# Twelve token tiles: all layer norms and transposes first, then all K and V projections

## The reference

```python
x = x + layernorm(attn(layernorm(x)))
x = x + layernorm(ffn(layernorm(x)))

# attn: 32 heads of 128 dimensions, ONE key head and ONE value head
Q = x @ Wq.T;  K = x @ Wk.T;  V = x @ Wv.T      # Wk, Wv: (128, 4096)
Qr, Kr = rope(Q), rope(K)
out = sliding_window(sigmoid scores, normalised; window 512, half overlapping, blended)
return out @ Wo.T
# ffn: x @ base_W.T + routed low-rank terms (8 experts, top 2, rank 16)
```

## Time and profile before

| | us |
|---|---|
| median of 3 runs | 2727.24 |
| lowest, highest | 2717.52, 2794.48 |
| the profiled execution | 2714.36 |
| its span on the slowest core (core 1) | 2712.8 |
| spans of the 8 cores | 2693.8 to 2712.8 |
| TensorE busy, of the span | 2003.1 (74%) |
| ScalarE busy | 659.5 (24%) |
| VectorE busy | 578.5 (21%) |

### The profile page before, as it was taken

How to read it: one execution, slowest core, us unless ns; L and a number is a source line. 1 busy time by engine, 2 the same in 40 slices (tenths; PEclk the granted TensorE clock), 3 DMA queues, 4 the chain that set the end, 5 groups by cost and what they waited for, 6 DMA issues and landing times.

```text
span 2712.8 us, 50094 instructions; the slowest of 8 cores (2693.8 to 2712.8 us)
## 1 busy us (share of the span) xinstructions
PE 2003.1 (74%) x20000; PEld 1720.9 (63%) x20000; DVE 578.5 (21%) x1656; ACT 659.5 (24%) x1159; POOL 135.7 (5%) x194
## 2 busy tenths in 40 slices
PE   1444599999998777788899999931222699999910
PEld 1333499999976555566688888831212588888810
DVE  1222222222213334433200000034332000000045
ACT  1434211111125554545211111132332011111122
POOL 1000000000000000000000000001101100000000
PEclk9556799999996888867899999965555799999965
DMA  9522044565561000000356475512111755755445
GB/s 182 121 94 93 32 63 63 70 84 66 63 78 18 2 2 2 2 2 2 18 72 85 63 92 65 75 50 62 41 53 32 89 73 67 91 69 72 73 140 217
DMA packets 228592, 179.01 MB, mean 66 GB/s; under 512 B 18960, under 2 KB 222736, under 8 KB 222736
## 3 DMA queue, kind: packets, MB, share of 16 engines
q0 software_dynamic: 217568, 113.35, 33.3%
q1 hardware_dynamic: 10800, 62.45, 6.4%
HBM read 263.97 MB, written 25.17 MB: 107 GB/s over the span
## 4 chain that ended last, share of the span: by engine, by line
PE 67%; issue 9%; DVE 9%; ACT 7%; DMA 6%; POOL 1%; DVEq 1%; ACTq 0%; POOLq 0%; SPq 0%
PE ps_all L814 17%; PE ps_all L670 17%; PE ps_all L455 16%; PE ps_all L557 7%; DVE bn L264 4%; PE ps_all L505 2%; DMA xre<-x_ext 2%; ACT sig L519 2%; DMA wvT_s<-wvT 2%; ACT xt_stage L283 2%; PE ps_all L296 2%; DMA x1re<-x_scratch 1%; DVE bl L593 1%; PE ps_all L351 1%; PE ps_all L356 1%
## 5 line engine op out<-in xcount | busy, mean ns | idle before, releaser
L814 PE MATMUL ps_all<-slab,ln2T 128*128 128x256 bf16 x4096 | 463.7, 273 | 22.2 <-DMA brider<-b_all 22.2
L455 PE MATMUL ps_all<-slab,ln1T_own 128*128 128x256 bf16 x4096 | 467.9, 273 | 0.7 <-ACT krT L380 0.7
L670 PE MATMUL ps_all<-slab,attn_T 128*128 128x256 bf16 x4096 | 449.6, 273 | 1.0 <-ACT attn_T L631 1.0
L814 PEld LDWEIGHTS ps_all<-slab,ln2T 128*128 128x128 bf16 x4096 | 402.0, 98 | 69.9 <-issue 22.4
L670 PEld LDWEIGHTS ps_all<-slab,attn_T 128*128 128x128 bf16 x4096 | 401.8, 98 | 48.8 <-issue 1.2
L455 PEld LDWEIGHTS ps_all<-slab,ln1T_own 128*128 128x128 bf16 x4096 | 395.4, 98 | 44.3 <-issue 0.8
L519 ACT ACTIVATE sig<-ps_all,kbias_s 128x512 bf16<-128x512 f32 x384 | 225.5, 719 | 244.6 <-PE ps_all L505 244.3
L557 PE MATMUL ps_all<-v_sb,sig 128*128 128x128 bf16 x2048 | 237.7, 245 | 45.4 <-DVE bl L593 40.4
L557 PEld LDWEIGHTS ps_all<-v_sb,sig 128*128 128x128 bf16 x2048 | 224.8, 125 | 57.0 <-issue 56.9
L567 PE MATMUL ps_all<-onesc,sig 128*128 128x1 bf16 x2048 | 232.5, 190 | 0.0
L567 PEld LDWEIGHTS ps_all<-onesc,sig 128*128 128x128 bf16 x2048 | 193.7, 101 | 0.0
(11 more groups left out here) (90 smaller groups left out, 1585.7 us busy)
## 6 DMA issues: line engine op xcount, KB each, us to landing
slab<-wqT POOLq DMA_DIRECT2D x16, 2048.0 KB, 18.6
slab<-woT POOLq DMA_DIRECT2D x16, 2048.0 KB, 17.0
slab<-baseT POOLq DMA_DIRECT2D x16, 2048.0 KB, 14.7
xstage<-x_ext SPq DMA_DIRECT2D x12, 2048.0 KB, 7.7
out<-outstage SPq DMA_DIRECT2D x8, 2048.0 KB, 7.9
xre<-x_ext POOLq DMA_DIRECT2D x8, 1024.0 KB, 8.2
x_scratch<-x1b SPq DMA_DIRECT2D x8, 1024.0 KB, 3.9
x1re<-x_scratch SPq DMA_DIRECT2D x8, 1024.0 KB, 9.7
```

The lines of the kernel that those rows point to most:

```text
L455: return e.matmul(reg, ln1T_own[:, d, t * 128:(t + 1) * 128], slabs[par][:, d, :], start=(d == 0), stop=(d == 31))
L670: return e.matmul(reg, attn_T[:, d, t * 128:(t + 1) * 128], slabs[par][:, d, :], start=(d == 0), stop=(d == 31))
L814: return e.matmul(reg, ln2T[:, d, t * 128:(t + 1) * 128], slabs[par][:, d, :], start=(d == 0), stop=False)
```

## The change

The one loop becomes two: all 12 a(ti) stand first, then all 12 b0(ti). `xt_stage` moves up by 8192 bytes, so that it no longer lies on `ln1T_halo`; it now lies on the first bytes of `v_sb` and on the rotary buffers `km1` and `km2`, which b0 alone writes. From L386 on, line numbers shift (the query tables' L393 becomes L392).

```diff
-    xt_stage  = sb("xt_stage", (128, D), BF16, FREG + 24576)
+    xt_stage  = sb("xt_stage", (128, D), BF16, FREG + 32768)
...
-    for ti in range(NTX + 1):
-        if ti >= 1:
-            emit_b0(ti - 1)
-        if ti < NTX:
-            emit_a(ti)
+    for ti in range(NTX):
+        emit_a(ti)
+    for ti in range(NTX):
+        emit_b0(ti)
```

## The result

Over ten executions each, the changed kernel has a median of 2659.3 us (lowest 2652.1) and the kernel before one of 2724.5 us (lowest 2716.4). The ratio is 0.9777, with a 95% interval of 0.9737 to 0.9817: faster, though this interval alone leaves open whether by 2%. By it the change makes the kernel faster by 66 us, 2.4%. The forecast was 2640 us, 77.7 us less, with a range of 2618 to 2678.

What follows compares the result with a forecast made beforehand. It saw a chain of engines waiting on each other before the first query matmul: layer norms to 187.9 us, then K and V of 59.7, put that matmul at 247.7, not 325.42; 77.7 less gives 2640 us (2618 to 2678).

Steps and rivals of the forecast that it cites:

- The chain, and the statistics hidden: Layer norm stage: VectorE's next statistics run under ScalarE's apply and evacuations, so the period falls from 24.3 to 11.61 us.
- x late beside the slabs: Layer norms of tiles 2 to 5: x loads slowed by query weight slabs make ScalarE wait 13.2 us in all.
- The slabs 10 us later: Query weight loads: x takes its share earlier, so the second slab lands some 10 us after the former 96.2.
- K and V in one go: TensorE after the last transposes: first block 7.16 us, eleven more at 2.4 GHz of 4.78 each, 59.7 in all.
- The first query matmul: Start of the query projection: it comes at 247.7 us instead of 325.42.
- From there to the whole: Everything behind the first query matmul: order, waits and loads stay as before, so the whole 77.7 us gain reaches the end.
- the clock doesn't hold: Rival, K and V blocks: all run at 1.2 GHz, 36.3 us more, a gain of 41, 2676 us; chance 0.13.
- x becomes the bound: Rival, layer norm stage: x loads stay at contended speed to the end, up to 2751 us; chance 0.03.
- the loads aren't late: Rival, layer norm stage: x arrives in time, the 13.2 us of waits go, gain 90.9, 2627 us; chance 0.18.

## Why the prediction was right, point by point

- **The chain, and the statistics hidden.** Right. The period without late loads is 11.4 us (11.61 forecast). Held back, the statistics cost 48 us; moved alone, they bring 56.
- **x late beside the slabs.** Right in place and cause, and in size on core 1: 13.2 us forecast for tiles 2 to 5, of which 6.0 for tile 2; 15.7 measured on core 1, of which 7.0 for tile 2. The chosen 14 us a load, between bounds of 7.7 and 20, came as 14.0, 14.4 and 15.1. On the other cores the loads came less evenly, and the sum was 12.2 to 20.3 us; that it came so near on the core whose rows were read is in part luck. With the slabs away all of it goes. By the rule of the Trainium skill that a DMA engine goes round its queues packet by packet (page "DMA: Bandwidth & Descriptors", section "Queues, rings and completion order"), weighed in the prediction as one turn for each packet of the profile, a load would have taken an estimated 9 us. The trace doesn't agree with that weighing; whether a turn of the rule is one packet of the profile, no run here shows.
- **The slabs 10 us later.** Too small: the second slab was issued at 44.1 and landed 72.4 us later, at 116.5 on core 1, 20 us after the 96.2 of before. It was due only at the second slab's matmuls and nobody waited for the slab itself.
- **K and V in one go.** Right: first K matmul at 187.0 (187.2 forecast), and the clock is up from 1.1 us on. The first block took 5.4 us (192.41, where the next K matmul starts, less 186.97) instead of 7.2, because the step fell after 1.1 us, not five; the later blocks take 5.10 on the mean (from the transposition at 192.18 to the eleventh after it, at 248.32: 56.1 / 11) instead of 4.78. Of the difference most lies behind the second transposition, 0.39 us to the next K matmul (197.15 to 197.54, part of it marked as issue) where I had put one step of 0.056. Behind the first block it is 0.18 (192.23 to 192.41), behind ten later ones 0.39 each; why, no run shows. In the trace of before the next tile's layer norm stood there.
- **The first query matmul** on core 1: 249.2, forecast 247.7. Up to here the sum holds within 2 us, in part by luck: x is 2.5 us later than forecast, but the eleven periods are 2.6 us shorter together; the first K and V block is 1.7 us shorter, the eleven others together 3.5 longer.
- **From there to the whole: the step that failed.** "All of it reaches the end" holds for core 1, which gained 76 us at the first query matmul and 80 at its end. But 77.7 was the gain of the core whose rows I read, not that of the kernel. On cores 1 and 2 K waited for the V weights until 53.7 and 54.5; on the six others it started between 45.6 and 48.2, so they had reached the query projection 5 to 10 us ahead of core 1 and had less to gain: 69.5 us on the mean. Core 4, which began its query projection 7 us ahead of core 1, ended the profile of before level with it at 2712.8: its query projection took 483.0 us, core 1's 477.3, so which core ends last is decided later. So the measure of the stage is its mean over the cores. That accounts for 8.2 of the 11.7 us between 77.7 and 66.0; the other 3.5, not seen in the profiled executions, belong to executions without a trace and stay open.
- **Rivals.** That the clock doesn't hold and that x becomes the bound didn't happen; that the loads aren't late is what the kernel with late slabs made of it: 2627.6, where 2627 stood as the price. That the two agree so closely is in part chance: it is one execution, and its Q is 86.4 us earlier than before on the mean, where 90.9 stood.

## What to carry to other kernels

In a list that an engine runs strictly in order, look first for work that is ready but stands behind a wait: here three VectorE lines, moved ahead of the rotary step, carry four fifths of the gain of regrouping the whole loop. Packing such a chain brings its loads closer together, so look at once for what else fills the DMA engines then and isn't due yet. On several cores price a stage as its mean over the cores; the rows of the slowest core may hold a wait that the others don't have.

## What was not expected

- The record of the granted clock says nothing before its first entry, which on core 1 is a rise: at 59.4 us before, at 188.1 in the changed kernel. Ahead of it the tables of stretches read 1.00, in the changed kernel from 46.7 to 187.0, yet the first K matmuls at 186.97 step at 0.107 us, the 1.2 GHz level. The mean clock of core 1 rose from 0.836 to 0.878 partly by that; the step between matmuls is the surer reading.
- The second slab landed 72 us after its issue instead of 42.4, and x took 14 to 15 us a load instead of 7.7. The 72 holds time behind the first slab, which landed only at 87.1. From the landing of the V weights at 43.8 to 116.5 the two slabs took 36 us each, by this estimate, where the third slab, with no x beside it, took 19.2: x and the slabs each lost a factor near two when both queues were full.
